# Routing stage of an attention and mixture-of-experts kernel: operands of VectorE's small operations, the queue of the stores, and the order of ScalarE's step

## The reference, cut to what matters

```python
x = x + xattn(layernorm(x), ctx, ctx, Wq, Wk, Wv, bv, Wo, bo)   # ends in out @ Wo.T + bo
n = layernorm(x)                                                # per row, over 512
grouped = n.reshape(B, 32, 32, 512)                             # groups of t = 32 rows
logits  = einsum('bgtd,des->bgtes', grouped, controller)        # 32 x 4 = 128 per row
logits  = logits + linspace(0, 1e-6, 32)                        # breaks ties over t
perm    = (logits == max(logits, over t))                       # 0 or 1
dispatched = einsum('bgtd,bgtes->bgesd', grouped, perm)
inner   = relu(einsum('bgesd,desf->bgesf', dispatched, f1) + bias)
out     = einsum('bgesf,esfd->bgesd', inner, f2)                # and back by perm
x = x + einsum('bgesd,bgtes->bgtd', out, perm)
```

## Time and profile before

| | |
|---|---|
| median of 3 runs | 1375.56 us |
| profiled execution | 1373.08 us, span 1371.3 us |
| PE busy | 1207.8 us, 88% of the span |
| DVE busy | 926.3 us, 68% |
| ACT busy | 615.4 us, 45% |
| POOL busy | 583.7 us, 43% |
| DMA, queue of SP (q1) | 190.18 MB, 48.7% of 16 engines' span |
| DMA, queue of ACT (q10) | 18.88 MB, 3.8% |

### The profile page before, as it was taken

One profiled execution on the slowest core, in us unless ns is written; L12 is line 12 of the kernel. 1 busy time (PEld: TensorE's weight loads), 2 busy tenths in 40 slices (PEclk: granted clock), 3 DMA queues, 4 the chain that ended last, 5 costly groups with the idle time before them and its releaser, 6 DMA issues. The chain is left out here.

```text
span 1371.3 us, 29427 instructions
## 1 busy us (share of the span) xinstructions
PE 1207.8 (88%) x11456; PEld 828.3 (60%) x11456; DVE 926.3 (68%) x2198; ACT 615.4 (45%) x1143; POOL 583.7 (43%) x799
## 2 busy tenths in 40 slices
PE   5999999958889999999999999993699979887773
PEld 4888888844444555555555555532577768875552
DVE  6555555516566877787777777712699966549994
ACT  3222222202555655565565556651233336456661
POOL 0000000012645777776777777663466635302322
PEclk9999999986999999999999999996899986789986
DMA  6556555458543355555555555004877855553444
GB/s 233 214 213 213 212 213 213 153 186 188 117 106 73 91 112 123 122 119 124 124 124 125 124 124 124 17 16 125 290 229 229 259 179 162 216 188 87 117 120 146
DMA packets 163885, 210.76 MB, mean 154 GB/s; under 512 B 8881, under 2 KB 96561, under 8 KB 162737
## 3 DMA queue, kind: packets, MB, share of 16 engines
q1 hardware_dynamic: 149936, 190.18, 48.7%
q10 hardware_dynamic: 13824, 18.88, 3.8%
HBM read 131.17 MB, written 77.59 MB: 152 GB/s over the span
## 5 line engine op out<-in xcount | busy, mean ns | idle before, releaser
L718 ACT ACTIVATE p_t<-p_bank 128x512 f32<-128x512 f32 (+1 forms) x608 | 310.2, 588 | 225.6 <-PE p_bank L778 219.8
L759 PE MATMUL p_bank<-k_stack,q_stack 96*128 96x512 f32 (+3 forms) x768 | 284.9, 393 | 28.7 <-DMA ident<-in_ident 19.3
L664 DVE CUSTOM_DVE_ANT_0 tried<-p_bank,ban 128x128 bf16<-128x128 f32 (+3 forms) x512 | 236.6, 485 | 86.8 <-PE p_bank L759 86.6
L778 PE MATMUL p_bank<-q_stack,k_stack 97*128 97x512 f32 (+3 forms) x768 | 259.3, 359 | 11.4 <-ACT p_t L718 6.1
L759 PEld LDWEIGHTS p_bank<-k_stack,q_stack 96*128 96x128 f32 x768 | 145.9, 193 | 152.2 <-issue 64.1
L667 DVE TENSOR_REDUCE mx_a<-p_bank 128x1 f32<-128x512 f32 x256 | 175.9, 687 | 62.4 <-PE p_bank L759 61.0
L600 POOL TENSOR_SCALAR_AFFINE_SELECT p_t<-p_t 128x128 f32<-128x128 f32 (+2 forms) x288 | 102.2, 358 | 173.8 <-ACT p_t L718 166.5
L778 PEld LDWEIGHTS p_bank<-q_stack,k_stack 97*128 97x128 f32 x768 | 145.7, 191 | 43.0 <-ACT p_t L718 27.0
L796 PE MATMUL p_bank<-p_t,v_tile 128*32 128x512 f32 (+3 forms) x1536 | 163.8, 499 | 1.6 <-POOL p_t L600 1.1
L611 POOL TENSOR_TENSOR p_sum<-p_sum,p_t 128x512 f32<-128x512 f32 x128 | 160.1, 1287 | 0.5 <-ACT p_t L718 0.5
L584 POOL MEMSET k_stack<- 1x4096 f32 x3 | 10.4, 3506 | 302.0 <-POOLq L128 302.0
(11 more groups left out here) (121 smaller groups left out, 2323.1 us busy)
## 6 DMA issues: line engine op xcount, KB each, us to landing
q_stack<-q_hi SPq DMA_DIRECT2D x64, 256.0 KB, 6.7
k_stack<-k_hi SPq DMA_DIRECT2D x30, 512.0 KB, 9.4
f_sb<-in_f SPq DMA_DIRECT2D x5, 2048.0 KB, 8.3
x_in<-in_x SPq DMA_DIRECT2D x8, 1024.0 KB, 9.1
c_in<-in_ctx_t SPq DMA_DIRECT2D x8, 1024.0 KB, 11.1
k_hi<-k_hi_s SPq DMA_DIRECT2D x8, 1024.0 KB, 4.2
k_lo<-k_lo_s SPq DMA_DIRECT2D x8, 1024.0 KB, 6.4
v_rows<-v_out SPq DMA_DIRECT2D x8, 1024.0 KB, 4.3
```

Source lines behind the costliest of these rows:

```text
L664: dve.tensor_tensor_reduce(tried[:, TRIED[c]:TRIED[c] + w], got, ban0[:] if i == 0 else ban[:, CH - w:CH], 1.0, -3e38, ALU.add, ALU.max, t ...
L718: act.activation(pt[:, k % SLOTS_P, u * m:(u + 1) * m, 0:w], bank[:, SB + n % SR, 0:m * w].rearrange("p (m w) -> p m w", m=m), ACT.Exp, sc ...
L759: pe.matmul(bank[:, to, 0:w], qs[it % SLOTS][0:R, i * P // CH, h, i * P % CH:i * P % CH + P], ks[it % SLOTS][0:R, h, t0:t0 + w], start=Tru ...
L778: mm = pe.matmul(bank[:, SB + n % SR, h % m * w:(h % m + 1) * w], ks[slot][0:R + 1, h, j * P:(j + 1) * P], qs[slot][0:R + 1, sh, h, CH - w ...
```

## The change

Three things change in `route`:

1. VectorE's small operations. `add_tie` writes its result back into the PSUM bank that it reads, `find_best` and `choose` read it from there, and the SBUF tile `logits` is gone. `r1` and `rstd` are made by `tensor_scalar`, whose further operands are single columns read as per-partition scalars, in place of `scalar_tensor_tensor`, which streams two SBUF tensors. PE's routing matmuls therefore wait until `choose` of two tiles before is done (it was `add_tie`).
2. All stores (`x2`, `xn`, `pick_t`) are issued by SP, in a written order with the loads. `load` is split in `load_o`, issued in step s for tile s+3, and `load_x`. The `f1` loads are issued at the end of step 1. ACT issues no DMA in this block.
3. ACT's step begins with the square root of tile s-1 and the copy of the turned rows of tile s-2; before, the square root of tile s stood near the end.

```diff
@@ -882,7 +882,6 @@
         r0 = sb("r03", [P, 1], F32)
         r1 = sb("r13", [P, 1], F32)
         rstd = sb("rstd3", [P, 1], F32)
-        logits = sb("logits", [P, P], F32)
         best = sb("best", [P, GQ], F32)
         pick_t = sb("pick_t", [P, XR, P], F32)
         bank = ctx.enter_context(nc.psum_tensor("p3_bank", [P, 8, 512], F32))
@@ -926,10 +925,12 @@
             def _(sp):
                 sp.dma_start(wo_raw[:], a.wo_t.rearrange("(k p) n -> p k n", p=P)).then_inc(const_in, 16)
 
-                def load(i):
+                def load_o(i):
                     if i >= XR:
                         sp.wait_ge(o_lo_done, i - XR + 1)
                     sp.dma_start(o_raw[:, i % XR], o_src[i]).then_inc(o_loaded[i % XR], 16)
+
+                def load_x(i):
                     if i >= XR:
                         sp.wait_ge(x2_done, i - XR + 1)
                     sp.dma_start(xb[:, i % XR], x_src[i]).then_inc(x_loaded[i % XR], 16)
@@ -943,21 +944,42 @@
                     sp.dma_start(keep.raw[:, 1, h * n * P:(h + 1) * n * P].rearrange("p (i d) -> p i d", d=P),
                                  m.xn.rearrange("(i p) (k d) -> k p i d", p=P, d=P)[1, :, h * n:(h + 1) * n]).then_inc(keep.raw_in, 16)
 
-                load(0)
+                load_o(0)
+                load_x(0)
                 for dst, src in ((bo_row[:], a.bo.unsqueeze(0).broadcast_to([P, D])),
                                  (ident[:], a.ident), (ctl[:], a.controller.rearrange("(k p) n -> p k n", p=P)),
                                  (tie[:], a.tie_row.unsqueeze(0).broadcast_to([P, GT]))):
                     sp.dma_start(dst, src).then_inc(const_in, 16)
-                for i in range(1, NT):
-                    load(i)
-                    if i == XR:
+                for i in range(1, XR):
+                    load_o(i)
+                    load_x(i)
+                for s in range(NT + END):
+                    if s + XR < NT:
+                        load_o(s + XR)
+                    if 0 < s <= NT:
+                        sp.wait_ge(x2_done, s)
+                        sp.dma_start(x2_dst[s - 1], x2[:, (s - 1) % XR]).then_inc(x2_stored[(s - 1) % XR], 16)
+                        if s - 1 + XR < NT:
+                            load_x(s - 1 + XR)
+                    if s >= END:
+                        sp.wait_ge(pick_t_done, s - END + 1)
+                        sp.dma_start(m.pick[s - END], pick_t[:, (s - END) % XR]).then_inc(pick_stored[(s - END) % XR], 16)
+                    if 0 < s <= NT:
+                        sp.wait_ge(xn_done, s)
+                        sp.dma_start(xn_dst[s - 1], xn[:, (s - 1) % XR]).then_inc(xn_stored[(s - 1) % XR], 16)
+                    if s == 1:
                         sp.dma_start(keep.f1[:, 0], f1_src[0]).then_inc(f1_early, 16)
                         sp.dma_start(keep.f1[:, 1], f1_src[1]).then_inc(f1_early, 16)
                         sp.dma_start(keep.bias[:], a.bias_col).then_inc(f1_early, 16)
-                    if i == NT * 3 // 4:
+                    if s == NT * 3 // 4:
                         second_quarter(0)
                 second_quarter(1)
                 sp.wait_ge(f1_early, 48)
+                for u in range(XR):
+                    n = len(range(u, NT, XR))
+                    sp.wait_ge(x2_stored[u], 16 * n)
+                    sp.wait_ge(xn_stored[u], 16 * n)
+                    sp.wait_ge(pick_stored[u], 16 * n)
 
             @block.gpsimd
             def _(pool):
@@ -996,6 +1018,9 @@
                 o_part(1)
                 for s in range(NT + END):
                     mid, end = s - MID, s - END
+                    if 0 < s <= NT:
+                        act.wait_ge(chain, (s - 1) * CHAIN + 3)
+                        act.activation(sd[:], ve[:], ACT.Sqrt).then_inc(sd_done, 1)
                     if 0 <= mid < NT:
                         act.wait_ge(turned, mid + 1)
                         if mid >= 2:
@@ -1003,23 +1028,12 @@
                         act.copy(xn_t[:, mid % 2], bank[:, TB + mid % 2]).then_inc(xn_t_done, 1)
                     if 0 < s <= NT:
                         act.wait_ge(xn_done, s)
-                        act.dma_start(xn_dst[s - 1], xn[:, (s - 1) % XR]).then_inc(xn_stored[(s - 1) % XR], 16)
                         act.copy(keep.x_hi[:, s - 1], xn[:, (s - 1) % XR, 0:P]).then_inc(x_hi_done, 1)
                     if s + 2 < NT:
                         o_part(s + 2)
-                    if s < NT:
-                        act.wait_ge(chain, s * CHAIN + 3)
-                        act.activation(sd[:], ve[:], ACT.Sqrt).then_inc(sd_done, 1)
-                        act.dma_start(x2_dst[s], x2[:, s % XR]).then_inc(x2_stored[s % XR], 16)
                     if 0 <= end:
                         act.wait_ge(pick_turned, end + 1)
                         act.copy(keep.pick_tok[:, end], bank[:, DB + end % 2, 0:NE]).then_inc(pick_kept, 1)
-                        act.dma_start(m.pick[end], pick_t[:, end % XR]).then_inc(pick_stored[end % XR], 16)
-                for u in range(XR):
-                    n = len(range(u, NT, XR))
-                    act.wait_ge(x2_stored[u], 16 * n)
-                    act.wait_ge(xn_stored[u], 16 * n)
-                    act.wait_ge(pick_stored[u], 16 * n)
 
             @block.vector
             def _(dve):
@@ -1037,14 +1051,14 @@
                     dve.wait_ge(routed, i + 1)
                     if i > 0:
                         dve.wait_ge(pick_t_done, i)
-                    dve.tensor_tensor(logits[:].rearrange(grouped, g=GQ),
+                    dve.tensor_tensor(bank[:, LB + i % 2, 0:P].rearrange(grouped, g=GQ),
                                       bank[:, LB + i % 2, 0:P].rearrange(grouped, g=GQ),
                                       tie[:].unsqueeze(1).broadcast_to([P, GQ, GT]),
                                       ALU.add).then_inc(tie_done, 1)
 
                 def find_best(i):
                     dve.wait_ge(tie_done, i + 1)
-                    dve.tensor_reduce(best[:], logits[:].rearrange(grouped, g=GQ), AX.X,
+                    dve.tensor_reduce(best[:], bank[:, LB + i % 2, 0:P].rearrange(grouped, g=GQ), AX.X,
                                       ALU.max).then_inc(best_done, 1)
 
                 def choose(i):
@@ -1053,7 +1067,7 @@
                         dve.wait_ge(pick_turned, i - XR + 1)
                     dve.wait_ge(best_done, i + 1)
                     dve.tensor_tensor(pick_t[:, i % XR].rearrange(grouped, g=GQ),
-                                      logits[:].rearrange(grouped, g=GQ),
+                                      bank[:, LB + i % 2, 0:P].rearrange(grouped, g=GQ),
                                       best[:].unsqueeze(2).broadcast_to([P, GQ, GT]),
                                       ALU.is_equal).then_inc(pick_t_done, 1)
 
@@ -1081,8 +1095,8 @@
                 def apply(i):
                     dve.wait_ge(sd_done, i + 1)
                     link(i, 5, dve.reciprocal(r0[:], sd[:]))
-                    link(i, 6, dve.scalar_tensor_tensor(r1[:], r0[:], r0[:, 0:1], half[:], ALU.mult, ALU.mult))
-                    link(i, 7, dve.scalar_tensor_tensor(rstd[:], r1[:], 1.5, r0[:], ALU.add, ALU.mult))
+                    link(i, 6, dve.tensor_scalar(r1[:], r0[:], r0[:, 0:1], half[:, 0:1], ALU.mult, ALU.mult))
+                    link(i, 7, dve.tensor_scalar(rstd[:], r1[:], 1.5, r0[:, 0:1], ALU.add, ALU.mult))
                     if i >= XR:
                         dve.wait_ge(xn_stored[i % XR], (i // XR) * 16)
                         dve.wait_ge(turned, i - XR + 1)
@@ -1146,7 +1160,7 @@
                     if 0 <= mid < NT:
                         pe.wait_ge(xn_t_done, mid + 1)
                         if mid >= 2:
-                            pe.wait_ge(tie_done, mid - 1)
+                            pe.wait_ge(pick_t_done, mid - 1)
                         for k in range(KD):
                             mm = pe.matmul(bank[:, LB + mid % 2, 0:P], ctl[:, k], xn_t[:, mid % 2, k],
                                            start=(k == 0), stop=(k == KD - 1))
```

## The result

The changed kernel takes 1349.68 us, the median of six runs (1342.32 to 1355.46); the kernel before, with runs on the same chips added, 1370.18. The ratio is 0.984 with a 95% interval of 0.981 to 0.987. The forecast was 1357 us. The profiled execution took 1353.44 us, span 1351.7, 19.6 us less than before.

What follows compares the result with a forecast made beforehand. DVE, not PE, was taken to set the 4.88 us step, with 1.50 us waiting for POOL. Gains of 14.3 + 2.9 + 0.7 = 17.9 us led to 1357 us, 8 in 10 range 1348 to 1368.

Steps and rivals of the forecast that it cites:

- The wait for POOL: DVE's two-tensor SBUF operations wait 1.50 of 4.88 us for POOL; new operands would cut DVE's step to 3.50 us.
- The steady gain: Tile 5 to tile 31: 26 PE steps fall from 4.88 to 4.33 us, gaining 14.3 us (9.9 to 16.9).
- The stall: ACT's wait for o_raw behind the 4 MB weights: tile 5 begins earlier, gaining 2.9 us (0 to 5).
- The end: Block's end: ACT's DMA issues go and the last pick_t store leaves earlier, gaining 0.7 us (0 to 1.5).
- the ring: Loop from xn through ACT's copies and POOL's three operations to the next xn: 4.23 us, just under PE's step.
- Rival A: xn waits for POOL each step: DVE's step 4.56 us, gain 11.9 us, time 1364; chance 0.17.
- Rival B: Stores and loads in one queue lengthen the stall and the reading back: gain 12 us, time 1364; chance 0.13.
- Rival C: Column operations with scalars still wait for POOL: gain 3.6 us at the edges only, time 1372; chance 0.06.
- D: SP's order makes a loop through slow loads: period 5.34 us at 17 us landing, time 1388; chance 0.04.

Runs made afterwards that it cites:

- e1: The kernel before with only VectorE's new operands, stores and ACT's order as before: step 4.23 us, block 175.32 us, ratio to before 0.988.
- e6: The kernel before with POOL adding the bias row in one column instead of 512: step 4.23 us, block 175.10 us, ratio to before 0.989.
- e4: The changed kernel with stores issued by ACT again, loads and weights in the old order: step 4.23 us, block 174.00 us, ratio to before 0.991.
- e2: The changed kernel with VectorE's old operands, keeping stores on SP and ACT's new order: step 4.52 us, block 175.24 us, ratio to before 0.987.
- e8: The kernel before with ACT issuing the store of xn behind the copy o_hi: step 4.53 us, block 185.42 us, ratio to before 0.993.
- e7: The changed kernel with the two 2 MB expert weight loads cut into 16 pieces, one per step: block 158.64 us, ratio to before 0.978.
- e9: The kernel before with ACT's copy o_hi moved ahead of its wait for xn: step 4.23 us, block 176.40 us, ratio to before 0.988.

## Why the prediction was right

The forecast was 17.9 us off a median of 1375.56, 1357. Against the medians of the result (1370.18 and 1349.68) the gain is 20.5, and the block's is 22.35. So 1349.68 lies inside the range for 8 in 10 (1348 to 1368) and just below the forecast's own (1350 to 1366): the block gained 4.5 us more than the sum, and the six runs of the kernel before also have a median 5.4 us below that of the three. The mechanism held for the kernel after, and the sum was too small mostly at its end.

Step by step, against the block's own clock, which ran 2.1 us earlier:

- **The wait for POOL.** Right: `r1` 0.27, `rstd` 0.21, comparison 0.29 whatever POOL did, and PE is what is late next. e1 and e6 show it from both sides: the same POOL with other operands, the same operands with less of POOL.
- **The steady gain.** Forecast 14.3 us for 26 steps of 4.33; measured from the start of tile 5 to that of tile 31, 126.84 before and 111.66 after, 15.2. A step is 4.233: the routing matmuls, no longer behind a wait, take 0.81 to the next step and not the 0.92 of the earlier trace rows. Tile 5's own step took 5.84 (977.91 to 983.75), its matmuls 0.63 us at the lower clock after the stall.
- **The stall.** Forecast: `o_raw` of tile 5 at 975.5, tile 5 at 980.1. Measured, with the 2.1 us added: 975.5 and 980.0. The 1 us that I took off for the clock fell into the step above, so 4.0 us stand against 2.9.
- **The end.** This term was mis-sized: 0.7 forecast, 3.2 measured (start of tile 31 to the gathering, 16.65 and 13.46). 1.45 lie ahead of the end of the last comparison, for the most part in ACT's step. 1.7 lie behind it (4.3 us from its end to the gathering, now 2.6): the last `pick_t` store leaves earlier and the 1 MB reading back now stands behind it rather than ahead. e1 and e4, with stores on ACT, have ends of 13.0 and 12.7, the other kernels with stores on ACT 12.7 to 12.9; all kernels with stores on SP 9.9 to 10.1. How the 3 us divide between queue order and ACT's time was not tried.
- **What I had not seen.** I drew the ring for the kernel after (4.23 us) and not for the kernel before, whose 4.88 is that ring closed by `rstd`. So I would have valued the stores on SP at nothing in the middle, while e2, with them and ACT's order alone, has 4.52, and e8 reaches 4.53 by moving one issue. In the sum it did not matter, since PE's step covers both. In the middle (tile 5 to 31) the parts do not add: e1 gains 16.8 us there, e2 10.3, the change 15.2. Before and behind it they do: e2 alone gains 3.8 at the stall and 2.5 at the end, e1 next to nothing. So 16.5 + 16.6 make 22.35.
- **Rival A** has its mechanism: L1104 waited for POOL to 1.21 us at the stall. In the middle of the change it takes 0.55: it begins when `x_lo` has 0.2 us to go, less than the 0.27 that the prediction let it spend beside POOL. But its absence there was not needed: in e1, e4 and e7 `xn` waited in most steps, up to 1.40, 1.39 and 1.60 us, and the step stayed 4.23. The rival's 4.56 took the full wait in every step; these were shorter in most. By the rule of the Trainium skill in "SBUF — State Buffer", "Who interferes with whom", an SBUF `tensor_scalar` can be shut out, and the trace agrees for 512 columns.
- **Rival B** failed: in the middle `o_raw` landed in a median of 3.5 us and at most 5.9, `xb` in 3.8 (2.8 before); POOL waited 1.74 us once for `xb` at the reading back, and no step grew. Five kernels with stores on ACT (e1, e4, e6, e8, e9) waited there for `o_raw`, 1.7 to 3.6 us, the kernel before did not; why is open. Nor was there much to lose at the weights: `x2` and `xn` of tile 1 landed 14.0 and 13.9 us after their issue on SP's queue, but 12.7 and 10.8 on ACT's in the kernel before, where both landed behind the weights too. The prediction had them pass there.
- **Rival C** is refuted by `r1` and `rstd` at 0.27 and 0.21, **D** by the step of 4.23.

## What to carry to other kernels

When an engine waits for another in every step, follow the wait once around: if the releasing work hangs on what the waiting engine produced a step ago, the step is the length of that ring, and one issue or copy within it costs its time in every step. Such a ring can be shortened (e8), opened by order (e9) or freed of the wait (e1), and these gains do not add, because the next engine (here PE, at 4.23) bounds the step in the end. Gains at other places, here at the stall and at the block's end, do add. A large load put in one piece into a queue that feeds a pipeline stalls it even where the bandwidth suffices, and in pieces, one per step, it need not.

## What the runs showed of the hardware

- A one-column `scalar_tensor_tensor` waits out a POOL operation like a wide one: 1.04 us instead of 0.22 (e6, e9). Each further scalar read from SBUF costs about 0.06 us (0.16, 0.22 and 0.27 us for none, one and two).
- A wide `tensor_scalar` between SBUF tensors waits for POOL as well, and then ends 0.28 to 0.29 us after it, though it takes 0.55 alone. POOL is held in its turn: `x_lo` took 0.64 to 0.65 us in place of 0.46 where it began while such an `xn` was still running (at 976.00 in the change, 1041.82 in e1).
- One queue carried 336 GB/s of loads and stores at a share of 0.99 with no wait on PE (e7, 960 to 1000 us); single loads of `xb` and `o_raw` then landed in a median of 5.2 and 5.0 us, against 3.8 and 3.5 in the middle of the change.
